# Attention scores in float32r: stacks of two parts on half the TensorE array each, in place of three bf16 parts on the whole array

## The chip, the cores and the metric

The kernel runs on one core of a Trainium2 chip. The metric is the device time of one execution in microseconds (us). Engines are named as in the profile: PE is TensorE's matmul, PEld its weight load, DVE is VectorE, ACT ScalarE, POOL GpSimd, SP SyncE, whose queue issues most DMAs.

## What is computed

The input x holds 64 sequences of 64 channels by 256 positions, in float32. Four residual stages follow each other, each behind a layer norm over the last axis: attention with a band mask (layer 0), a feed-forward with ternary weights and a norm clip (`ff0`), attention with rotary positions on q and k (layer 1), and a feed-forward of width 1024 with 4-bit weights and low-rank terms. The scores of an attention are, shortened:

```python
scores = jnp.einsum('bqhd,bkhd->bhqk', q, k) / jnp.sqrt(jnp.asarray(d, q.dtype))   # 8 heads of d = 8
band = jnp.abs(idx[:, None] - idx[None, :]) <= local_size                          # layer 0: 64
scores = jnp.where(band[None, None], scores, neg)
attn = jax.nn.softmax(scores, axis=-1)
o = jnp.einsum('bhqk,bkhd->bqhd', attn, v).reshape(n, t, e)
```

Layer 1 has the same form over 256 keys without a band, with q and k turned: `t * cos(pos) + rot * sin(pos)`, where `rot` swaps the two halves of each head's 8 channels and negates one.

## The kernel before

Two sequences make a *pair*, laid over the 128 partitions; there are 32 pairs and 16 heads per pair (`HPP`). All of x stays in SBUF (`X`). Each attention layer is one software pipeline over the pairs, written out by hand for each engine: an `iteration(r)` walks the 16 heads of pair r, and beside them works on pairs r+1 (scores and row maxima), r+2 (v, stacks), r+3 (q and k projections) and r-1 (heads turned back, output projection). `Fori` loops run over rounds of `RING` = 3 pairs. Engines are joined by semaphores only, and PE takes its instructions in the order that `tensor_attention.iteration` gives.

Per head the scores are computed twice. `score_head` (L408) computes them with the queries on the partitions, so that DVE takes the row maxima (L1031). `shifted_head` (L425) computes them again with the keys on the partitions and the row maximum subtracted in the same matmul; ACT takes the exponential of that (`exp_head`, L687) into `probs`, and in layer 0 POOL sets the places outside the band to zero (`mask_group`, L1234). `values_group` (L443) multiplies four heads' probabilities with V, in four column strips of the array (L459). In layer 0 a score also starts from a band matmul of 384 columns (L418), which adds a large negative number outside the band. The windows are 192 keys per block of 128 queries in layer 0 (`WIN`), 256 in layer 1.

To keep float32 precision, q and k are split into three bf16 parts (`PARTS` = 3): ACT rounds the first (`high_part`, L699 and L704), DVE takes the rest (L1041) and POOL rounds and subtracts the others (`split`, L1201 to L1208). All nine products of parts are stacked along the contraction: 9 x 8 = 72 rows, and a matmul on `Qs` and `Ks` sums them. The score matmul takes 96 rows (some of them zero), the shifted one 128: rows 96 to 98 hold -1 in `Ks` and the three parts of the row maximum in `Qs`. SP lays the stacks out (`lay_out`, L341 and L344) and replicates them (`replicate`, L355 and L357); `shift_rows` (L366) brings the maxima, which `split_max` (L935 to L941), a transpose on PE (L490) and ACT (L741) have prepared. In layer 1 the rotated rows are taken out of the projection by two ACT instructions of 64 partitions (L716). Four values groups, projections (L470), v (L479), transposes (L501, L512) and the transposes of the maxima (L490) stand between the heads on PE.

At the start of the program the weights of the last feed-forward are prepared on PE by pairs of matmuls that share a bank: 128 rows of dequantised weights, then 16 rows of the low-rank term (L578/L579, L583/L584).

## Time and profile before

| | us |
|---|---|
| median of 3 runs | 1431.23 |
| lowest, highest | 1430.2, 1431.35 |
| profiled execution: span | 1429.4 |
| PE busy | 1315.2 (92%) |
| PEld busy | 910.0 (64%) |
| DVE busy | 955.8 (67%) |
| ACT busy | 874.6 (61%) |
| POOL busy | 716.5 (50%) |

The span runs from the first to the last instruction of the profiled execution, and is the only time shown of that execution. Layer 0 lies between about 45 and 570 us, the first feed-forward up to about 655, layer 1 up to about 1190, the last feed-forward to the end. A busy PE says that matmuls are in flight, not that the array works at its peak; durations of matmuls in the trace include a latency, so the distance from one start to the next tells the cost in a row of them. PEld overlaps PE.

### The profile page before, as it was taken

The page shows a single profiled execution, that of the slowest core. Times are in us where ns is not written, and L with a number is a line of the kernel's source. Part 1 is how long each engine was busy: PE and PEld are TensorE (multiplying, and loading weights), DVE is VectorE, ACT ScalarE, POOL GpSimd, SP SyncE. Part 2 cuts the span into 40 slices and gives each one's busy share as a digit, 9 for nine tenths or more (in the row PEclk, how much of TensorE's full clock was granted, in tenths as well). Part 3 has the DMA queues.
Part 4 walks back from the last instruction along what each step waited for, and adds up shares of the span by engine and source line. Part 5 has one row for each costly group of instructions (what it writes and reads, how often), then busy time and mean ns, then how long its engine had stood idle before and what let it go on. Part 6 is the DMA issues. An engine that isn't in the chain of part 4 may idle for free.

```text
span 1429.4 us, 37785 instructions
## 1 busy us (share of the span) xinstructions
PE 1315.2 (92%) x11332; PEld 910.0 (64%) x11332; DVE 955.8 (67%) x2156; ACT 874.6 (61%) x1909; POOL 716.5 (50%) x1292
## 2 busy tenths in 40 slices
PE   1999999999999998882799999999999989999998
PEld 1666777777777776571466666666666655766675
DVE  6438878787888787468888888888888872111110
ACT  1147676666666667563488888888888875122211
POOL 6336777777777776404555655656656511010000
PEclk9869999999999999995799999999999999999999
DMA  8314444444344443001434444444444410000000
GB/s 243 78 36 95 103 100 90 96 100 100 90 96 100 100 90 87 6 12 37 92 91 104 105 95 103 103 97 104 102 97 107 93 41 1 15 30 15 15 15 29
DMA packets 90797, 111.18 MB, mean 78 GB/s; under 512 B 15056, under 2 KB 82384, under 8 KB 83056
## 3 DMA queue, kind: packets, MB, share of 16 engines
q1 hardware_dynamic: 83184, 103.38, 31.9%
q10 hardware_dynamic: 7552, 7.02, 1.7%
q8 instruction: 34, 0.56, 0.2%
q14 instruction: 27, 0.22, 0.1%
HBM read 16.52 MB, written 4.19 MB: 14 GB/s over the span
## 4 chain that ended last, share of the span: by engine, by line
PE 62%; POOL 11%; issue 11%; DVE 8%; ACT 2%; ACTq 1%; DMA 1%; POOLq 1%; SPq 1%; DVEq 1%
PE bank L459 10%; PE bank L420 8%; PE bank L652 8%; PE bank L643 8%; PE bank L436 7%; PE bank L418 5%; PE bank L470 4%; DVE row_max L1031 3%; PE bank L501 3%; POOL rot L1216 2%; PE bank L614 2%; POOL Qp L1205 2%; PE bank L490 1%; POOL k_rest L1221 1%; POOL q_rest L1201 1%
## 5 line engine op out<-in xcount | busy, mean ns | idle before, releaser
L1031 DVE TENSOR_REDUCE row_max<-bank 128x2 f32<-128x384 f32 (+1 forms) x1024 | 599.6, 617 | 148.5 <-PE bank L420 146.8
L687 ACT ACTIVATE probs<-bank 128x384 f32<-128x384 f32 (+1 forms) x1024 | 534.4, 542 | 161.8 <-PE bank L436 155.0
L420 PE MATMUL bank<-Ks,Qs 96*128 96x192 bf16 (+1 forms) x2048 | 372.1, 264 | 13.5 <-DMA Ks<-Ks 8.4
L436 PE MATMUL bank<-Qs,Ks 128*128 128x192 bf16 (+1 forms) x2048 | 367.1, 261 | 13.6 <-ACT probs L687 12.5
L1234 POOL TENSOR_SCALAR_AFFINE_SELECT probs<-probs 128x256 f32<-128x256 f32 (+1 forms) x512 | 257.2, 526 | 175.1 <-ACT probs L687 156.3
L420 PEld LDWEIGHTS bank<-Ks,Qs 96*128 96x128 bf16 x2048 | 189.3, 99 | 122.8 <-issue 37.8
L459 PE MATMUL bank<-probs,V 128*32 128x192 f32 (+1 forms) x4096 | 249.0, 361 | 3.7 <-POOL probs L1234 2.4
L436 PEld LDWEIGHTS bank<-Qs,Ks 128*128 128x128 bf16 x2048 | 188.9, 98 | 40.1 <-ACT probs L687 23.9
L418 PE MATMUL bank<-band,ident 128*128 128x384 bf16 x512 | 169.2, 331 | 1.0 <-ACT out_bias L840 0.5
L459 PEld LDWEIGHTS bank<-probs,V 128*32 128x32 f32 x4096 | 107.4, 109 | 82.7 <-issue 41.8
L1171 DVE TENSOR_TENSOR X<-bank,X 128x256 f32 (+1 forms) x32 | 13.6, 425 | 184.6 <-PE bank L652 184.6
L1216 POOL TENSOR_TENSOR rot<-rot,rope 128x256 f32<-128x256 f32 x64 | 46.9, 732 | 132.1 <-ACT rot L716 132.1
L643 PE MATMUL bank<-Ks,up_w 128*128 128x512 f32 x256 | 111.8, 592 | 0.0
L1302 POOL TENSOR_TENSOR X<-X,down_b 128x256 f32 x32 | 23.1, 751 | 169.2 <-DVE xn L1006 169.2
L470 PE MATMUL bank<-xn,att_w 128*128 128x256 f32 x192 | 66.2, 431 | 37.7 <-DVE xn L1006 37.7
L733 ACT ACTIVATE heads_sb<-bank 128x512 f32<-128x512 f32 x128 | 75.6, 591 | 27.3 <-PE bank L459 27.3
L643 PEld LDWEIGHTS bank<-Ks,up_w 128*128 128x128 f32 x256 | 48.4, 190 | 56.8 <-issue 56.4
L501 PE MATMUL bank<-ident,heads_sb 128*128 128x128 f32 x512 | 77.9, 275 | 2.0 <-ACT heads_sb L733 2.0
L901 ACT ACTIVATE probs<-bank,up_b 128x512 f32<-128x512 f32 x32 | 22.0, 687 | 85.8 <-PE bank L643 85.8
L716 ACT ACTIVATE rot<-bank,att_b 64x256 f32<-64x256 f32 x128 | 60.0, 469 | 15.2 <-PE bank L470 12.1
L901 ACT ACTIVATE Qs<-bank,up_b 128x512 f32<-128x512 f32 x32 | 22.0, 687 | 76.1 <-PE bank L643 76.1
L501 PEld LDWEIGHTS bank<-ident,heads_sb 128*128 128x128 f32 x512 | 59.2, 142 | 12.3 <-issue 4.4
(128 smaller groups left out, 1776.9 us busy)
## 6 DMA issues: line engine op xcount, KB each, us to landing
Ks<-Ks SPq DMA_DIRECT2D x64, 576.0 KB
Qs<-Qs SPq DMA_DIRECT2D x128, 192.0 KB
Qs<-Qp SPq DMA_DIRECT2D x192, 64.0 KB
Ks<-Kp SPq DMA_DIRECT2D x192, 64.0 KB
side<-in_ctx SPq DMA_DIRECT2D x64, 128.0 KB, 2.0
X<-in_x ACTq DMA_DIRECT2D x4, 1024.0 KB, 10.4
out<-X SPq DMA_DIRECT2D x8, 512.0 KB, 2.9
Qs<-max_rows SPq DMA_DIRECT2D x128, 12.0 KB
```

The source lines that it names most:

```text
L418: nc.tensor.matmul(dst[:, 0:2 * win], ident16[:, :], band16[:, :], start=True, stop=False)
L420: last = nc.tensor.matmul(dst[:, blk * win:(blk + 1) * win], Qs[0:SHIFT_ROW, pair[1], h, blk * P:(blk + 1) * P], Ks[0:SHIFT_ROW, pair[1], ...
L436: last = nc.tensor.matmul(dst[:, blk * win:(blk + 1) * win], Ks[:, pair[1], h, blk * P:(blk + 1) * P], Qs[:, pair[1], h, start(blk):start( ...
L459: last = nc.tensor.matmul(dst[32 * j:32 * j + 32, first:first + win], V[:, pair[1], blk, head, :], probs[:, head % 8, blk * win:(blk + 1) ...
L470: nc.tensor.matmul(job_bank[b][:, 0:T], w[:, weight, :], source, start=True, stop=True).then_inc(s[f"{b}_filled"], 1)
L501: last = nc.tensor.transpose(job_bank["A"][:, (blk * 2 + g) * P:(blk * 2 + g + 1) * P], heads_sb[:, half, g * T + blk * P:g * T + (blk + 1 ...
L643: last = nc.tensor.matmul(bank[2 + hb % 2][:, :], up_w[:, blk, hb * P:(hb + 1) * P], xT[:, cu, blk, :], start=(blk == 0), stop=(blk == 1))
L652: last = nc.tensor.matmul(bank[4 + j % 2][:, 0:T], hidden[cu][:, hb, j * P:(j + 1) * P], down_w[:, hb, :], start=(hb == 0), stop=(hb == HB ...
L687: nc.scalar.activation(probs[:, h % 8, 0:2 * win], exp_bank[h % 2][:, 0:2 * win], ACT.Exp, scale=SCALE).then_inc(s["exped"], 1)
L733: nc.scalar.activation(heads_sb[:, half, :], pv_bank[:, :], ACT.Copy).then_inc(s["heads_out"], 1)
L1031: nc.vector.tensor_reduce(row_max[:, pair[1], h, :], bank_of(pair, h)[:, 0:2 * win].rearrange("p (b k) -> p b k", b=2), AX.X, ALU.max).the ...
L1234: return nc.gpsimd.affine_select(out=part, in_=part, compare_op=ALU.is_ge, fill=0.0, base=base, pattern=[[0, 4], [-sign, width]], channel_ ...
```

## The change

1. `PARTS` is 2: q and k are split into a first part, rounded to float32r on writing (11 mantissa bits are kept), and the rest in float32. The four products of parts take 4 x 8 = 32 rows. An even head and an odd head now share a slot of `Qs` and `Ks` (float32r, eight slots a pair): even heads in partitions 0 to 63, odd heads in 64 to 127. The last two rows of each half (62 and 63) hold -1 in `Ks` and the two parts of the row maximum in `Qs`.
2. A score block takes 62 rows and a shifted block 64 rows of one half. `score_and_shift` issues them block by block in turn, the score of head h of the next pair and the shifted scores of head h^1 of this pair, so that they lie in different halves. Before the first block PE waits for DVE's maxima and for ACT's exponential together. ACT and the values groups follow the swapped order.
3. The stacks are laid out by eight DMAs of 128 KB, spread over the partitions, and `replicate` is gone; `shift_rows` takes two DMAs a half pair. In layer 0 the DMAs wait for the reading of the projection, without POOL's `split`. `Ks` is cleared to -1 by one memset, and POOL's memset of its shift rows is gone.
4. The split of the maxima has two instructions in place of four and moves in layer 0 from DVE to POOL; its transpose is float32 with 32 columns in place of bf16 with 48.
5. In layer 1 a second projection per q and k gives the rotated rows (two more weight blocks), and ACT takes them out with one instruction of 128 partitions in place of two of 64.
6. Buffers of the later stages are other aliases of memory.

On PE in layer 0, two heads in the middle of a pair (L418/L433 the band, L420/L410 the score, L436/L419 the shifted scores, L501/L510 transposes). Before:

```order
L418 MATMUL bank1<-band16,ident16 128x384
L420 MATMUL bank1<-Ks,Qs 128x192 x2
L436 MATMUL bank2<-Qs,Ks 128x192 x2
L501 MATMUL bank6<-ident,heads_sb 128x128 x4
L418 MATMUL bank5<-band16,ident16 128x384
L420 MATMUL bank5<-Ks,Qs 128x192 x2
L436 MATMUL bank3<-Qs,Ks 128x192 x2
```

And in the changed kernel, around a values group (L466) and a transpose of the maxima (L499):

```order
L433 MATMUL bank5<-band16,ident16 128x384
L410 MATMUL bank5<-Ks,Qs 128x192
L419 MATMUL bank3<-Qs,Ks 128x192
L410 MATMUL bank5<-Ks,Qs 128x192
L419 MATMUL bank3<-Qs,Ks 128x192
L466 MATMUL bank4<-probs,V 32x192 x8
L499 MATMUL bank6<-ident,max_parts 32x128
L433 MATMUL bank0<-band16,ident16 128x384
L410 MATMUL bank0<-Ks,Qs 128x192
L419 MATMUL bank2<-Qs,Ks 128x192
```

The number of matmuls per head is the same; the four blocks alternate, and the band matmul stands between the groups of four as before.

On SP, one iteration in the loop of layer 0 (`Qp`, `Kp` are the parts, `max_rows` the turned maxima). Before:

```order
L325 DMA side<-in_ctx 128x256
L341 DMA Qs<-Qp 8x16x256 x3
L344 DMA Ks<-Kp 8x16x256 x3
L366 DMA Qs<-max_rows 3x16x128
L355 DMA Qs<-Qs 24x4096 x2
L357 DMA Ks<-Ks 72x1x4096
L366 DMA Qs<-max_rows 3x16x128
```

And now, with the instructions that take the waits:

```order
L326 DMA side<-in_ctx 128x256
L301 REGISTER_ALU
L301 ISA
L334 DMA Qs<-Qp 16x8x256 x4
L301 REGISTER_ALU
L334 DMA Ks<-Kp 16x8x256 x4
L283 ISA
L364 DMA Qs<-max_rows 2x8x128 x2
L283 REGISTER_ALU
L364 DMA Qs<-max_rows 2x8x128 x2
```

Eight DMAs now stand ahead of the first shift rows in place of six, and none between the two sets of shift rows in place of three.

The core of the diff:

```diff
-PARTS = 3
-SPLIT_ROWS = PARTS * PARTS * HD
-SHIFT_ROW = 96
+PARTS = 2
+SLOTS = HPP // 2
+GROUP = P // 2
+ROWS_D = GROUP // HD
+SHIFT_ROW = GROUP - PARTS
...
-        Qs = sb("Qs", [P, RING, HPP, T], bf16)
-        Ks = sb("Ks", [P, RING, HPP, T], bf16)
+        Qs = sb("Qs", [P, RING, SLOTS, T], fp32r)
+        Ks = sb("Ks", [P, RING, SLOTS, T], fp32r)
...
+            def spread(tensor, u, product, part):
+                dst = bass.AP(tensor, u * SLOTS * T + product * row, [[ROWS_D * row, 2 * HD], [T, SLOTS], [1, T]])
+                return e.dma_start(dst, part)
...
                 for i in range(PARTS):
-                    e.dma_start(Ks[COPY_ROW + i * HD:COPY_ROW + (i + 1) * HD, u, :, :],
-                                Kp[:, u, i, :]).then_inc(s[f"k_in{u}"], 16)
-
-            def replicate(pair):
...
+                    for j in range(PARTS):
+                        spread(q_stack, u, i * PARTS + j, Qp[:, u, i, :]).then_inc(s[f"q_in{u}"], 16)
...
-                e.dma_start(Qs[SHIFT_ROW:SHIFT_ROW + PARTS, pair[1], half * HEADS:(half + 1) * HEADS, :],
-                            max_rows[:, half, :]).then_inc(s[f"max_in{half}"], 16)
+                for odd in range(2):
+                    first = odd * GROUP + SHIFT_ROW
+                    e.dma_start(Qs[first:first + PARTS, pair[1], half * SLOTS // 2:(half + 1) * SLOTS // 2, :]
+                                .bitcast(fp32),
+                                max_rows[odd * PARTS * HEADS:(odd + 1) * PARTS * HEADS, half, :]
+                                ).then_inc(s[f"max_in{half}"], 16)
...
+            def score_block(pair, h, blk):
+
+                rows = slice(h % 2 * GROUP, h % 2 * GROUP + SHIFT_ROW)
+                return nc.tensor.matmul(bank_of(pair, h)[:, blk * win:(blk + 1) * win],
+                                        Qs[rows, pair[1], h // 2, blk * P:(blk + 1) * P],
+                                        Ks[rows, pair[1], h // 2, start(blk):start(blk) + win],
+                                        start=(l == 1), stop=(l == 1 or blk == 1))
+
+            def shifted_block(pair, i, blk):
+
+                h = i ^ 1
+                rows = slice(h % 2 * GROUP, h % 2 * GROUP + GROUP)
+                return nc.tensor.matmul(exp_bank[i % 2][:, blk * win:(blk + 1) * win],
...
+            def score_and_shift(ahead, pair, h):
...
+                    wait_some(e, s["exped"], n - 1)
+                if active(ahead):
+                    score_block(ahead, h, 0)
+                if active(pair):
+                    shifted_block(pair, h, 0)
+                if active(ahead):
+                    score_block(ahead, h, 1).then_inc(s["scored"], 1)
+                if active(pair):
+                    shifted_block(pair, h, 1).then_inc(s["shifted"], 1)
...
+                if turned is not None:
+                    nc.tensor.matmul(job_bank[b][:, T:2 * T], w[:, turned, :], source, start=True, stop=True)
...
-                half = P // 2
-                for here, there in ((slice(0, half), slice(half, P)), (slice(half, P), slice(0, half))):
-                    nc.scalar.activation(rot[here, 2 * n + 1, :], job_bank[bk][there, 0:T], ACT.Identity,
-                                         bias=b[there, column:column + 1]).then_inc(s["turned"], 1)
+                nc.scalar.activation(rot[:, 2 * n + 1, :], job_bank[bk][:, T:2 * T], ACT.Identity,
+                                     bias=b[:, column:column + 1]).then_inc(s["turned"], 1)
...
+            engine.tensor_scalar(parts[:, :, 0, :].bitcast(fp32r), src, 1.0, None, ALU.mult).then_inc(high, 1)
+            wait_apart(e, (high, num(pair) + 1))
+            engine.tensor_tensor(parts[:, :, 1, :], src, parts[:, :, 0, :],
                                  ALU.subtract).then_inc(s[f"max_parts{half}"], 1)
...
-            def split(name, pair, parts, rest, mid, done):
+            def low_part(name, pair, parts, rest):
```

## Rows read from the trace of the kernel before

**Rows 1.** The page, busy time of each engine with its share and instructions.

```profile
span 1429.4 us, 37785 instructions
...
PE 1315.2 (92%) x11332; PEld 910.0 (64%) x11332; DVE 955.8 (67%) x2156; ACT 874.6 (61%) x1909; POOL 716.5 (50%) x1292
```

**Rows 2.** Busy time by stretch: length, engines, granted clock (PEclk), DMA share, GB/s.

```profile
60.00:84.00 24.00, 24.00 (x67) 16.60 (x68) 0.00 (x0) 2.39 (x4) 0.00 (x0) 0.50 0.03 4
202.40:361.40 159.00, 155.02 (x1683) 114.37 (x1682) 127.28 (x332) 109.47 (x250) 117.27 (x211) 1.00 0.43 96
839.40:991.60 152.20, 149.22 (x1502) 99.95 (x1501) 132.14 (x251) 130.11 (x281) 90.59 (x180) 1.00 0.45 101
```

**Rows 3.** The same stretch of layer 0, L436 alone: PE, PEld.

```profile
202.40:361.40 159.00, 52.61 (x322) 28.73 (x320) 1.00 0.43 96
```

**Rows 4.** PE in order of time, layer 0: start, length, line, operands, count.

```profile
303.26 0.32 PE L418 MATMUL bank<-band,ident 128*128 128x384 bf16 x1
303.42 0.33 PE L420 MATMUL bank<-Ks,Qs 96*128 96x192 bf16 x2
303.59 0.33 PE L436 MATMUL bank<-Qs,Ks 128*128 128x192 bf16 x2
303.76 0.32 PE L418 MATMUL bank<-band,ident 128*128 128x384 bf16 x1
...
304.08 0.33 PE L436 MATMUL bank<-Qs,Ks 128*128 128x192 bf16 x2
304.34 0.86 PE L459 MATMUL bank<-probs,V 128*32 128x192 f32 x16
305.13 0.44 PE L512 MATMUL bank<-ident,normed 128*128 128x128 f32 x2
305.41 0.61 PE L479 MATMUL bank<-att_w,xn 128*128 128x128 f32 x4
```

**Rows 5.** PE in order of time, layer 1.

```profile
905.05 0.38 PE L420 MATMUL bank<-Ks,Qs 96*128 96x256 bf16 x2
905.27 0.38 PE L436 MATMUL bank<-Qs,Ks 128*128 128x256 bf16 x2
905.58 1.07 PE L459 MATMUL bank<-probs,V 128*32 128x256 f32 x16
906.58 0.39 PE L420 MATMUL bank<-Ks,Qs 96*128 96x256 bf16 x2
```

**Rows 6.** PE's waits: us in total, times, longest.

```profile
PE bank L420 <- DMA Ks<-Ks: 8.4, 1, 8.4
```

**Rows 7.** PE in order of time, preparation of weights.

```profile
66.32 0.80 PE L583 MATMUL bank<-ident,ff 128*128 128x128 f32 x2
67.04 0.79 PE L584 MATMUL bank<-probs 16*128 16x128 f32 x2
```

**Rows 8.** Groups of weight loads by form: busy us, mean ns of one.

```profile
L420 PEld LDWEIGHTS bank<-Ks,Qs 96*128 96x128 bf16 x2048 | 189.3, 99 | 122.8 <-issue 37.8 <-DVE row_max L1031 11.5 <-DMA Ks<-Ks 8.7
...
L643 PEld LDWEIGHTS bank<-Ks,up_w 128*128 128x128 f32 x256 | 48.4, 190 | 56.8 <-issue 56.4
```

**Rows 9.** SP's queue in order of time, layer 1, one iteration.

```profile
899.96 2.02 SPq L341 DMA_DIRECT2D Qs<-Qp  x3
902.02 1.93 SPq L344 DMA_DIRECT2D Ks<-Kp  x3
904.09 0.77 SPq L366 DMA_DIRECT2D Qs<-max_rows  x1
```

**Rows 10.** PE in the same iteration, the ninth head's shifted scores.

```profile
907.92 0.38 PE L436 MATMUL bank<-Qs,Ks 128*128 128x256 bf16 x2
```

**Rows 11.** The page, DMA issues: count, KB each, median us to landing.

```profile
side<-in_ctx SPq DMA_DIRECT2D x64, 128.0 KB, 2.0
```

**Rows 12.** The chain that ended last, ahead of layer 1's first score.

```profile
664.60 0.91 POOL Qp L1205
...
665.59 0.67 POOL Qp L1208
...
674.43 6.06 DMA Ks<-Ks
```

243 lines of the change are left out of this document (98 added, 145 removed).

## The prediction

> **What bounds the kernel now.** I read the page's busy line first [rows 1]: PE is busy for 92% of the span, no other engine for more than 67%. The table by stretches [rows 2] splits that. Its last two stretches hold ten pairs each (in the first 320 weight loads of L436, 32 a pair [rows 3]), so a pair takes 15.90 us in layer 0 and 15.22 in layer 1. PE is busy for 97% and 98% of them, at full granted clock. Behind it stand DVE with 12.7 us a pair in layer 0 and 13.2 in layer 1, and ACT with 10.9 and 13.0. Then I read PE in order of time. In layer 0 the band matmul comes every 0.50 us: 0.16 for its 384 columns, 0.17 for the two score matmuls, 0.17 for the two shifted ones, nothing between [rows 4]. In layer 1 two matmuls of 256 columns take 0.22, a head 0.44 [rows 5]. That is one column a cycle at 2.4 GHz. The longest wait of a score matmul on anything is a single one of 8.4 us, at a ramp [rows 6]. So what shortens or lengthens PE's row decides, until DVE's 13.2 us or the SP queue takes over.
>
> **The score and shifted matmuls.** Each now uses half the rows, and the order puts a score block on one half beside a shifted block on the other. No row shows a float32r matmul, nor two row halves at once, so I bound them. Plain f32 with 256 columns takes two instructions of 0.216 us (L459's sixteen run in four rounds of four, from 905.58 to 906.46 [rows 5]). If that is four products of operand parts, one product is a quarter, 0.108, as bf16. The same rounds show four matmuls in disjoint column strips running together. If row halves do so too, a head's two block pairs take 0.22 in layer 1 against 0.44, and 0.16 to 0.19 in layer 0 against 0.335. If either fails it is twice that. I take the good case, since L459's rounds are the nearest rows; the bad case is a rival.
>
> **Changing the array's form.** When PE goes from full-array matmuls to L459's 32 columns and back, the next instruction comes late. In layer 0 the last L436 pair starts at 304.08 and lasts 0.17, so L459 was due at 304.25 and starts at 304.34: 0.09 lost. Its rounds of 0.16 end at 304.99 and L512 starts at 305.13 (0.14 lost); its two then take 0.28 where two of L479 take 0.22 (0.06, a weight load that nothing hides) [rows 4]. In layer 1 it is 0.09 in and 0.12 out [rows 5]. The preparation shows it for rows: f32 matmuls alternate between 128 and 16 rows at a granted clock of 0.50, 1.2 GHz [rows 2], and come every 0.72 us [rows 7], where two of L479's 0.11 at half speed are 0.44; the other 0.28 is one change of form. The bf16 stacks of 96 and 128 rows alternate without loss [rows 4]; a half of 62 or 64 rows I count as a form of its own.
>
> So in layer 0 each head now leaves and enters that form, because its band matmul is full-array. Out: 0.09, and 0.01 for a bf16 load. In: 0.09, and an exposed float32r load. A bf16 load lasts 99 ns, an f32 one 190 [rows 8]. I bound the exposed part by 0.05 (L512's) and 0.11 (the excess of 0.09 on top of a bf16 load's 0.01 to 0.02), and take 0.08. The four blocks go from 0.335 to between 0.40 and 0.49 us, middle 0.445: +0.11 a head, +1.8 us a pair, **+55 us** over 31 pairs; the ends are +32 and +77.
>
> The Trainium skill, page "TensorE: Matmul & The Clock Gate", section "Weight-path perf modes", says that weights load fast when there are 128 of them and the input is not FP32; the 99 against 190 ns agrees. An estimate by it: if float32r counts as FP32 this term takes its upper end, +77; if it loads as bf16 does, exposed 0.01, it is +12.
>
> In layer 1 there is no band, but projections, transposes and values groups stand between the heads. Along the loop's order I count 20 changes of form a pair against 11 before (the transpose of the maxima now has the values group's 32 columns). That is 9 x 0.09 = +0.8, and ten entries with a load of 0.08, less the bf16 loads, +0.7. Blocks: 16 x 0.22 = -3.5. The rotated projections are two more f32 matmuls, four instructions of 0.216: +0.9. Sum -1.1 us, a pair of 14.1, still above DVE's 13.2. ACT's four half-height L716 become two full ones, off the path.
>
> **What moves on SP.** The stacks now take eight DMAs and no replication. Three L341 took 2.02 us to issue and three L344 1.93 [rows 9], so about 0.65 each. Behind them queues the shift row of the second half, now two DMAs. Before, it was issued 4.13 us after the iteration began (899.96 to 904.09 [rows 9]) and used at 907.92, the ninth head [rows 10]. Now its second DMA is issued after 8 x 0.65 + 0.77 = 6.0 us, and with the 2.0 us that the side load takes to land [rows 11] it is there at 8.0, when layer 1's ninth head is due at 7.96 - 0.55 = 7.4. PE waits 0.5 or so. The landing takes 3.8 us at most (904.09 to 907.92, with no wait), the wait then 2.4. In layer 0, with 17.7 us a pair, the head is due near 8.8: no wait. Layer 1: -1.1 + 0.5 = -0.6 a pair, **-18 us** over 30, ends -33 and +39.
>
> **The ramps.** In the chain before layer 1's first score [rows 12], POOL's L1205 and L1208 go, for q and for k (2 x 1.58 = 3.2 us), and the replication's 6.06; the larger layout DMAs give back some 2. With 3 at the program's start: **-10 us**, ends -15 and -5. Costed at nothing: DVE's split of the maxima in layer 0 moves to POOL, which loses 1.6 us of work each for q and k and gains four small operations. It stands there behind a mask group with about one head to spare before PE asks; without that, PE would wait for it once a pair. The changed aliases of the later stages move no work.
>
> **Sum.** The profiled execution's span is 1429.4 us [rows 1], the runs' median 1431.2, so 1.8 lies around the span. 1429.4 + 55 - 18 - 10 = 1456.4, and 1.8 more: **1458 us**. Its own range, by the ends and +12 as the lowest first term, is 1395 to 1540.
>
> **Rivals.**
> - *Changing form costs little here*, for instance since one half works while the other drains. Layer 0's blocks fall to 0.175: -0.16 x 16 x 31 = -79. Layer 1 loses the added 1.5 too, but its first half cannot go below SP's 8.0 us, so I give it -1.0 x 30 = -30. With the ramps **1312**. The balance point: my gains elsewhere are 28 us, 0.056 a head of layer 0, so the kernel is faster if a way out and in costs under 0.22 us, where I take 0.27. For it: L459 in layer 1 shows 0.21. Against it: the preparation pays in full, by rows.
> - *A four-byte moving operand streams at half speed.* Every f32 instruction in the rows takes two cycles a column, transposes too (L512, 0.28 less 0.06 for two of 128). Blocks then double: +0.17 x 16 x 31 = +84 and +3.5 x 30 = +105, less the SP wait's 15, on the forecast: **1632**. The skill's page "SBUF — State Buffer", section "A bandwidth-pool intuition that's wrong (but worth ruling out)", gives the moving operand's port as two bytes a lane and cycle, which is this rule.
> - *The change doesn't do what it says*: the halves run one after the other, each block 0.08 or 0.11. Same doubled price, **1632**. L459's overlap is in columns; no row shows one in rows.
> - *A lower clock.* In the preparation the clock stayed at 0.50 while forms alternated [rows 2]. If it did so in layer 0, a head's 0.33 us of columns would double and its two changes cost 0.28 each: +0.6 us, some +300 over 31 pairs. PE streams a larger share there, so I give it little.
>
> **Chances.** Forecast 0.55, of which 0.14 end faster (cheap end of the form change) and 0.04 the same; cheap changes 0.15; half speed 0.13; no overlap 0.12; lower clock 0.05. Faster 0.29, same 0.04 (within 0.2%, what a measurement of this kernel can tell from no change), slower 0.67. The range runs from 1380 to 1640: the forecast's own and both doubled prices. Outside lie most of the cheap case and the lower clock, 0.19.
>
> **What would show it.** In layer 0: band matmuls 0.6 us apart instead of 0.50, with 0.09 lost before and after the blocks; the two blocks of a pair starting a few ns apart, the next two 0.08 to 0.11 later. A spacing of 0.16 there is half speed; four evenly spaced starts are no overlap. Pairs of 17.7 us in layer 0 and 14.6 in layer 1, and there a wait of the ninth shifted head for the max_rows DMA. I am wrong if the band's spacing stays at 0.50 or below, or if a pair of layer 1 takes over 15.2.

## The result and the profile after

The changed kernel takes **1536.11 us** (median of four runs, 1535.57 to 1537.6) against 1430.72 us for the kernel before on the same chip. The ratio is 1.074, with a 95% interval of 1.0724 to 1.0755: slower by 105 us, where I had forecast 27. The profiled execution's span goes from 1429.4 to 1535.7 us. The page of the changed kernel, against [rows 1]:

```profile
span 1535.7 us, 37561 instructions
...
PE 1433.7 (93%) x11460; PEld 903.6 (59%) x11460; DVE 901.9 (59%) x1900; ACT 849.6 (55%) x1845; POOL 524.1 (34%) x1035
```

PE took the whole loss: it is busy 118 us longer, and every other engine is busy for less than before, POOL by 192 us. The busy time by stretch, against [rows 2] (length, PE, PEld, DVE, ACT, POOL, granted clock, DMA share, GB/s):

```profile
200.00:380.00 180.00, 178.40 (x1688) 106.91 (x1690) 113.10 (x252) 111.43 (x251) 96.23 (x210) 1.00 0.25 67
640.00:700.00 60.00, 53.55 (x383) 31.10 (x382) 20.98 (x53) 29.18 (x62) 25.52 (x54) 0.67 0.02 7
900.00:1100.00 200.00, 196.40 (x2000) 125.50 (x1998) 169.71 (x325) 156.67 (x338) 69.75 (x130) 1.00 0.29 79
```

PE is as full as before in both layers (99% and 98%), at full clock. New is the middle row, the end of layer 0: a granted clock of 0.67. PE in order of time in layer 0 of the changed kernel, against [rows 4] (start, length, line, operands, count):

```profile
305.05 0.34 PE L433 MATMUL bank<-band,ident 128*128 128x384 bf16 x1
305.32 0.35 PE L410 MATMUL bank<-Ks,Qs 62*128 62x192 f32 x1
305.32 0.35 PE L419 MATMUL bank<-Qs,Ks 64*128 64x192 f32 x1
305.51 0.27 PE L410 MATMUL bank<-Ks,Qs 62*128 62x192 f32 x1
305.52 0.27 PE L419 MATMUL bank<-Qs,Ks 64*128 64x192 f32 x1
305.72 0.48 PE L479 MATMUL bank<-rot,att_w 128*128 128x256 f32 x1
```

The two halves do overlap: score and shifted block start together, and the second pair of blocks is done 0.20 us after its start. What is paid lies between the instructions. The band matmul streams for 0.16 us and the blocks begin 0.27 after it (0.11 lost). A block pair is 192 columns, 0.08 at one column a cycle of 2.4 GHz, and the next follows after 0.19 (0.11 lost). After the second, the next full-array matmul starts 0.20 later (0.12 lost). So a head takes 0.16 + 0.11 + 0.08 + 0.11 + 0.08 + 0.12 = 0.66 us where it took 0.50. The weight loads of that head show the middle loss:

```profile
305.32 0.18 PEld L410 LDWEIGHTS bank<-Ks,Qs 62*128 62x128 f32 x1 [0.17 <-issue]
305.32 0.18 PEld L419 LDWEIGHTS bank<-Qs,Ks 64*128 64x128 f32 x1
305.43 0.19 PEld L410 LDWEIGHTS bank<-Ks,Qs 62*128 62x128 f32 x1
```

A float32r load lasts 0.18 to 0.19 us, as the f32 load of [rows 8], and the second load on the same half comes 0.11 after the first.

To place the rest I took from both traces the start of the first shifted matmul of some pairs, which cuts the span into stretches:

| stretch | before, us | after, us | difference |
|---|---|---|---|
| start to pair 0 of layer 0 | 90.2 | 108.0 | +17.8 |
| pair 0 to 4 | 64.4 | 75.3 | +10.9 |
| pair 4 to 31 | 431.1 | 492.1 | +61.0 |
| pair 31 to first transpose of `ff0` | 15.2 | 21.5 | +6.3 |
| to pair 0 of layer 1 | 92.8 | 92.2 | -0.6 |
| pair 0 to 4 | 69.3 | 71.6 | +2.3 |
| pair 4 to 31 | 415.1 | 420.8 | +5.7 |
| rest | 251.3 | 254.3 | +3.0 |

Between pairs 4 and 30 a pair takes 17.91 us in layer 0 (before 15.87) and 15.48 in layer 1 (before 15.21). The steady price is 31 x 2.04 = 63 us in layer 0 and 30 x 0.27 = 8 in layer 1. The other 35 us lie at the ramps: 17.8 before the first pair, 2.7 in the next four beyond their steady price, 12.2 at the end of layer 0 (5.9 of it in the row of pairs 4 to 31), and 2.4 elsewhere. (The 570 us given above for the end of layer 0 is too early. In the kernel before, its last scores stand at 584.5 us and its last shifted matmul starts at 596.7.)

The ramps show two things, a lower clock and changes of form that cost more at it. PE in order of time while layer 0's first pair is scored, first the changed kernel:

```profile
53.55 0.50 PE L433 MATMUL bank<-band,ident 128*128 128x384 bf16 x1
53.98 0.74 PE L410 MATMUL bank<-Ks,Qs 62*128 62x192 f32 x2
54.65 0.50 PE L433 MATMUL bank<-band,ident 128*128 128x384 bf16 x1
```

and the kernel before in the same phase:

```profile
52.65 0.34 PE L418 MATMUL bank<-band,ident 128*128 128x384 bf16 x1
52.83 0.33 PE L420 MATMUL bank<-Ks,Qs 96*128 96x192 bf16 x2
53.12 0.34 PE L418 MATMUL bank<-band,ident 128*128 128x384 bf16 x1
```

A head is 1.10 us there instead of 0.47. The blocks begin 0.43 us after the band matmul, whose 384 columns are 0.32 us at the 1.2 GHz level and 0.16 at 2.4. The clock is the smaller part of the 0.63 us, because a little earlier the kernel before scores at that level too:

```profile
47.96 0.53 PE L418 MATMUL bank<-band,ident 128*128 128x384 bf16 x1
48.28 0.53 PE L420 MATMUL bank<-Ks,Qs 96*128 96x192 bf16 x2
48.60 0.97 PE L470 MATMUL bank<-xn,att_w 128*128 128x256 f32 x2
```

Its head takes 0.64 us (47.96 to 48.60). The other 0.46 of the 1.10 come with the change's blocks: the changes of form and the exposed load at half clock. In the trace of before the clock is granted at 1.00 from 49.3 to 59.5 us and again from 93.7; in the changed kernel first from 121.2. At the end of layer 0 it falls to 0.50 from 653.7 to 674.2 and twice more up to 701.5, where before it was lost for 3.4 us only.

### The profile page after: what moved, and what is told of

Read it like the earlier page. It is cut to its first block, busy times and chain, and to the rows that moved or that the text cites. A ratio compares the mean times of both kernels' runs of the same rounds, so it can differ in the third digit from the quotient of the medians.

```text
span 1535.7 us, 37561 instructions
## 1 busy us (share of the span) xinstructions
PE 1433.7 (93%) x11460; PEld 903.6 (59%) x11460; DVE 901.9 (59%) x1900; ACT 849.6 (55%) x1845; POOL 524.1 (34%) x1035
## 4 chain that ended last, share of the span: by engine, by line
PE 82%; DVE 6%; POOL 4%; issue 3%; ACT 3%; ACTq 1%; SPq 0%; POOLq 0%; DVEq 0%; DMA 0%
PE bank L410 20%; PE bank L466 14%; PE bank L661 7%; PE bank L479 7%; PE bank L652 7%; PE bank L433 6%; PE bank L510 4%; POOL probs L1221 3%; PE bank L419 3%; PE bank L478 2%; DVE row_max L1035 2%; PE bank L488 2%; PE bank L623 2%; PE bank L521 2%; ACT probs L697 1%
## 5 line engine op out<-in xcount | busy, mean ns | idle before, releaser
L410 PE MATMUL bank<-Ks,Qs 62*128 62x192 f32 (+1 forms) x2048 | 467.9, 322 | 28.4 <-ACT probs L697 14.2
L419 PE MATMUL bank<-Qs,Ks 64*128 64x192 f32 (+1 forms) x2048 | 461.1, 320 | 2.4 <-ACT probs L697 2.4
L410 PEld LDWEIGHTS bank<-Ks,Qs 62*128 62x128 f32 x2048 | 305.8, 192 | 249.2 <-issue 134.5
L419 PEld LDWEIGHTS bank<-Qs,Ks 64*128 64x128 f32 x2048 | 299.2, 190 | 8.8 <-ACT probs L697 6.4
L466 PE MATMUL bank<-probs,V 128*32 128x192 f32 (+1 forms) x4096 | 253.9, 367 | 7.8 <-POOL probs L1221 4.4
L433 PE MATMUL bank<-band,ident 128*128 128x384 bf16 x512 | 176.2, 344 | 0.5 <-ACT out_bias L848 0.5
L466 PEld LDWEIGHTS bank<-probs,V 128*32 128x32 f32 x4096 | 108.7, 111 | 72.4 <-POOL probs L1221 8.2
L943 POOL TENSOR_SCALAR max_parts<-row_max 128x16 fp32r<-128x16 f32 x128 | 32.5, 254 | 345.0 <-DVE row_max L1035 339.7
L909 ACT ACTIVATE ff<-bank,up_b 128x512 f32<-128x512 f32 x64 | 44.0, 687 | 163.5 <-PE bank L652 163.5
L661 PE MATMUL bank<-down_w,ff 128*128 128x256 f32 x512 | 112.6, 381 | 0.8 <-ACT ff L909 0.8
L652 PE MATMUL bank<-probs,up_w 128*128 128x512 f32 x256 | 112.7, 597 | 0.0
L661 PEld LDWEIGHTS bank<-down_w,ff 128*128 128x128 f32 x512 | 96.6, 190 | 15.8 <-ACT ff L909 1.6
L510 PE MATMUL bank<-ident,heads_sb 128*128 128x128 f32 x512 | 82.8, 285 | 1.6 <-ACT heads_sb L741 1.4
L652 PEld LDWEIGHTS bank<-probs,up_w 128*128 128x128 f32 x256 | 48.8, 192 | 57.7 <-issue 57.3
## 6 DMA issues: line engine op xcount, KB each, us to landing
ff<-in_down_q ACTq DMA_DIRECT2D x1, 1024.0 KB, 10.8
```

The lines of the kernel that those rows point to most:

```text
L410: return nc.tensor.matmul(bank_of(pair, h)[:, blk * win:(blk + 1) * win], Qs[rows, pair[1], h // 2, blk * P:(blk + 1) * P], Ks[rows, pair[ ...
L419: return nc.tensor.matmul(exp_bank[i % 2][:, blk * win:(blk + 1) * win], Ks[rows, pair[1], h // 2, blk * P:(blk + 1) * P], Qs[rows, pair[1 ...
L433: nc.tensor.matmul(bank_of(ahead, h)[:, 0:2 * win], ident16[:, :], band16[:, :], start=True, stop=False)
L466: last = nc.tensor.matmul(dst[32 * j:32 * j + 32, first:first + win], V[:, pair[1], blk, head, :], probs[:, head % 8, blk * win:(blk + 1) ...
L510: last = nc.tensor.transpose(job_bank["A"][:, (blk * 2 + g) * P:(blk * 2 + g + 1) * P], heads_sb[:, half, g * T + blk * P:g * T + (blk + 1 ...
L652: last = nc.tensor.matmul(bank[2 + hb % 2][:, :], up_w[:, blk, hb * P:(hb + 1) * P], xT[:, cu, blk, :], start=(blk == 0), stop=(blk == 1))
```

## The experiments

My theory was that the loss is made of changes of form (the array emptied before and after the blocks, and a four-byte load that nothing hides) and of lost clock at the ramps. The rivals: the half-array float32r blocks are slow by themselves; the load has no part in it; the ramps are long for another reason. "Pair" below is the time between pairs 4 and 30 in the profiled run, divided by 26, as above.

### 1. Without the band matmul

```diff
-                    if l == 0:
-                        nc.tensor.matmul(bank_of(ahead, h)[:, 0:2 * win], ident16[:, :], band16[:, :],
-                                         start=True, stop=False)
...
-                                        start=(l == 1), stop=(l == 1 or blk == 1))
+                                        start=True, stop=True)
```

> The changed kernel without the layer 0 band matmul (left out: the mask in the scores of layer 0, so that its row maximum is taken over the whole window). Theory, form changes: each change of form costs a drain of about 0.11 us and an exposed load of about 0.1 us; without the band the half-array pairs follow each other as in layer 1 (spacing 0.12 us) and a head falls from 0.66 to 0.24-0.30 us, a layer 0 pair from 17.97 to 12-13.5 us, where VectorE (11.3 us a pair) is near; time about 1536 - 31 x 5 = 1380 us (1360 to 1410). Rival, the float32r blocks themselves are slow (0.19 us for two halves whatever stands before them): a head stays at 0.38 us or more, a pair at 13.5-15 us, time 1430 to 1470 us.

Measured: 1542.95 us, ratio 1.0781 (1.0739 to 1.0822). Less work, and no gain. The table by stretches of this kernel says why; the first row is layer 0's steady part, the others two pieces of it:

```profile
200.00:380.00 180.00, 163.01 (x1459) 106.15 (x1458) 105.50 (x240) 100.58 (x241) 90.72 (x201) 0.79 0.23 63
330.70:340.90 10.20, 8.51 (x104) 5.63 (x102) 7.64 (x17) 6.75 (x17) 5.77 (x13) 1.00 0.33 84
341.00:368.00 27.00, 26.72 (x170) 16.78 (x162) 12.00 (x27) 12.38 (x28) 10.91 (x24) 0.50 0.21 57
```

The clock alternates between its two levels all through layer 0. DVE has 11.1 us of work a pair here (105.50 us in 180, a pair being 19.02). At full clock it does 7.64 us in 10.20, so a pair takes 15; at half clock 12.00 in 27, so 25. Where the clock is full, the blocks behave as the theory says:

```profile
371.41 0.35 PE L410 MATMUL bank<-Ks,Qs 62*128 62x192 f32 x1
...
371.60 0.27 PE L410 MATMUL bank<-Ks,Qs 62*128 62x192 f32 x1
371.60 0.38 PE L419 MATMUL bank<-Qs,Ks 64*128 64x192 f32 x2
371.72 0.27 PE L410 MATMUL bank<-Ks,Qs 62*128 62x192 f32 x1
...
371.83 0.27 PE L410 MATMUL bank<-Ks,Qs 62*128 62x192 f32 x1
```

After the change of form the second block pair comes 0.19 later, the third and fourth 0.11 to 0.12: the load is exposed once per entry and hidden from then on. The theory holds for the blocks, and my forecast of the time missed by 160 us. Most of that is the clock, which it left out, but not all: even at full clock a pair took 15 us, with PE busy for 8.51 of 10.20 us, where my 1380 us needs 12.9. By an estimate from these rows that is 31 x 2.1 = 65 of the 160.

### 2. The same in the kernel before

> The kernel before without the layer 0 band matmul (left out: the mask in the scores of layer 0). Here every matmul of a head has the full form, so only the band's own 0.16 us can go: a pair falls by 16 x 0.16 = 2.6 us from 15.89 to 13.3 us, the time by 31 x 2.6 = 80 us to 1350 us (1340 to 1365). If a band matmul cost more than its stream in this kernel too, the fall is over 100 us and the comparison with the changed kernel does not show form changes.

The edit is the same, on L418 and L420. Measured: 1392.22 us, ratio 0.9734 (0.9716 to 0.9752), **faster than both kernels**, and 42 us above my forecast. A pair falls by 1.26 us and not by 2.56, since PE now waits (146.41 us busy of 160, against 155.02 of 159 [rows 2]). The clock is at 1.00 from 116.7 to 540.0 us. So the band can go without losing the clock where the other matmuls fill the whole array.

### 3. The halves with bf16 loads

```diff
+            def rows_of(h):
+                return slice(h % 2 * 64, h % 2 * 64 + 64)
...
-                                            Qs[0:SHIFT_ROW, pair[1], h, blk * P:(blk + 1) * P],
-                                            Ks[0:SHIFT_ROW, pair[1], h, start(blk):start(blk) + win],
+                                        Qs[rows_of(h), pair[1], h, blk * P:(blk + 1) * P],
+                                        Ks[rows_of(h), pair[1], h, start(blk):start(blk) + win],
```

(the shifted blocks take `rows_of(h + 1)`; order and waits are those of the change)

> The kernel before with its blocks cut to 64 rows of the array and issued block by block between the halves as in the change (left out: the products in the other half of the stacks). Theory, form change = drain + four-byte load: the drain of 0.11 us stays twice a head, the exposed load (bf16 loads take 99 ns instead of 190) goes down to 0.05 us or less: a layer 0 head of 0.50-0.58 us, a pair of 15.5-16.7 us. Rival, the exposed load does not depend on the type: a head of 0.65 us and a pair of 17.9 us as in the changed kernel. Rival, only the load costs: a head below 0.40 us and a pair under 14.5 us.

Measured, in one execution: 1435.75 us, a pair of 16.21 us in layer 0 and 14.62 in layer 1. PE in order of time, layer 0 of this kernel:

```profile
303.93 0.33 PE L433 MATMUL bank<-band,ident 128*128 128x384 bf16 x1
304.19 0.25 PE L413 MATMUL bank<-Ks,Qs 64*128 64x192 bf16 x1
304.19 0.25 PE L420 MATMUL bank<-Qs,Ks 64*128 64x192 bf16 x1
304.28 0.24 PE L413 MATMUL bank<-Ks,Qs 64*128 64x192 bf16 x1
...
304.46 0.34 PE L433 MATMUL bank<-band,ident 128*128 128x384 bf16 x1
```

and its weight loads of the next head:

```profile
304.72 0.09 PEld L413 LDWEIGHTS bank<-Ks,Qs 64*128 64x128 bf16 x1 [0.17 <-issue]
304.73 0.09 PEld L420 LDWEIGHTS bank<-Qs,Ks 64*128 64x128 bf16 x1
304.74 0.10 PEld L413 LDWEIGHTS bank<-Ks,Qs 64*128 64x128 bf16 x1
```

The 0.10 before and the 0.10 after the blocks are there, but the second block pair follows after 0.09 instead of 0.19, and the second load on a half comes 0.02 after the first instead of 0.11. A head takes 0.53 us. So changes of form alone cost layer 0 0.34 us a pair over the kernel before, because the overlapped blocks pay for them; the other 1.70 us of the change's 2.04 come with the float32r stacks, and the exposed load is most of it (16 x 0.11 = 1.8, where every head has one). A small part of that difference may be the rest of the change, since this kernel keeps the three-part splits on the other engines.

Its start is long as well. Pair 0's first shifted matmul stands at 100.0 us (90.2 before, 108.0 with the change), the clock is first granted at 104.2, and the scores of the first pair take 16.5 us (10.5 before, 20.2 with the change). So more than half of what the start loses comes without float32r.

### 4. More full-array work at the ramps

```diff
+                        times = 3 if not active(pair) else 2 if isinstance(pair[0], int) and num(pair) == 0 else 1
+                        for t in range(times):
                             nc.tensor.matmul(bank_of(ahead, h)[:, 0:2 * win], ident16[:, :], band16[:, :],
-                                             start=True, stop=False)
+                                             start=True, stop=t < times - 1)
...
+                elif l == 0 and h > 3 and active(pair):
+                    e.wait_ge(s["maxed"], PAIRS * HPP)
+                    for _ in range(2):
+                        nc.tensor.matmul(score_bank[h % 2][:, 0:2 * win], ident16[:, :], band16[:, :],
+                                         start=True, stop=True)
```

> The changed kernel with its band matmul issued three times a head in layer 0's score-only iterations, twice in the first iteration that also shifts, and two extra band matmuls a head into idle score banks in layer 0's last iteration: full-array work in the stretches where the granted clock was low. Nothing is left out. Theory, the ramps are lost by the clock: the clock is granted at 1.00 by the first pair's scores or soon after 105 us instead of at 121, and does not fall at 653 us; 20 to 40 us come back, time 1496 to 1520 us. Rival, the ramps are long because half-array heads are longer there at either clock: no gain, 1536 to 1545 us, since the extra matmuls only add work.

Measured: 1541.4 us, the median of four executions of which one took 4035.23 us (why isn't known) and the others 1535.96 to 1543.42; the span of the profiled one is 1534.1. The clock moved but the time did not. It was granted from 62.6 us to 76.2, in the weight preparation, again from 124.0 to 137.7, and came to stay at 141.1 instead of 121.2; from pair 0 to 4 took 80.3 us. At the end of layer 0 it stayed at 1.00 until 694.0, and pairs 4 to 31 took 483.5 us instead of 492.1. Those 8.6 us come with the clock, but it isn't shown that the extra matmuls kept it: the profiled executions of experiments 9 and 11, whose layer 0 is that of the change word for word, kept it to 680.3 and 671.0 us and took 483.7 both. As a test of the ramps the experiment is inconclusive.

### 5. Score, score, shifted, shifted

```diff
                 if active(ahead):
                     score_block(ahead, h, 0)
-                if active(pair):
-                    shifted_block(pair, h, 0)
-                if active(ahead):
                     score_block(ahead, h, 1).then_inc(s["scored"], 1)
                 if active(pair):
+                    shifted_block(pair, h, 0)
                     shifted_block(pair, h, 1).then_inc(s["shifted"], 1)
```

> The changed kernel with a head's four blocks in the order score, score, shifted, shifted instead of alternating. Theory, two halves overlap only where consecutive matmuls stand in different halves, and a load on one half hides behind a stream on the other: a layer 0 head grows by 0.05 to 0.15 us (pair 18.8-20.4 us), a layer 1 head by 0.1-0.2 us (pair 17-18.5 us), time 1610 to 1690 us. Rival, the array takes the next half's load early whatever the order: same time within 10 us.

Measured, in one execution: 1536.03 us, a pair of 17.94 and 15.53 us. The rival was right. PE in order of time in this kernel:

```profile
304.40 0.33 PE L433 MATMUL bank<-band,ident 128*128 128x384 bf16 x1
304.65 0.35 PE L410 MATMUL bank<-Ks,Qs 62*128 62x192 f32 x1
304.66 0.35 PE L419 MATMUL bank<-Qs,Ks 64*128 64x192 f32 x1
304.85 0.27 PE L410 MATMUL bank<-Ks,Qs 62*128 62x192 f32 x1
```

The first shifted block starts beside the first score block although two score blocks stand before it in the program. It starts 7 ns after it and not 3 (medians from 200 to 380 us), the only mark that the new order left. Alternating block by block, which the change wrote out with care, does nothing for the time; that the blocks lie in different halves does all.

This run also gives a price for the clock by chance: here it was granted at 143.6 us instead of 121.2, and pairs 0 to 4 took 83.9 us instead of 75.3; it was kept until 662.4, and pairs 4 to 31 took 485.7 instead of 492.1, the way to `ff0` 16.9 instead of 21.5. The edit changes no steady pair, so 22 us at half clock at the start cost 8.6, and the fall at the end of layer 0 cost 11. The moment of the grant needn't be the edit's doing. With layer 0 as in the change, it came at 121.4 us in experiment 11 (pairs 0 to 4 in 75.8 us) and at 144.5 in experiment 9 (84.0 us). So how the 35 us are spread over the ramps belongs in part to the one execution that was profiled; the four executions of the change lie within 2.1 us of each other.

### 6. Half-array work twice

```diff
+                for blk in range(2):
+                    for rep in range(2 if l == 0 and active(ahead) and active(pair) else 1):
+                        if active(ahead):
+                            scored = score_block(ahead, h, blk)
+                        if active(pair):
+                            shifted = shifted_block(pair, h, blk)
```

> The kernel without bands (left out: the mask in the scores of layer 0), with every half-array block of layer 0 issued twice in place: more work, the same form. Without bands the granted clock alternated between 0.50 and 1.00 all through layer 0 and a pair took 19.1 us (about 15 at 1.00, 25 at 0.50). Theory, the clock is granted for how much the array does: with the doubled blocks it stays at 1.00, a head costs 4 x 0.12 = 0.48 us and a pair 15.5-17 us, time 1543 - 31 x 2.5 = 1465 us (1440 to 1500), faster with more work. Rival, the clock answers to full-array forms alone or the pair is bound elsewhere: the clock goes on alternating and the time rises to 1600-1680 us.

Measured: 1513.74 us, ratio 1.057 (1.0485 to 1.0656). Against experiment 1 it does twice the block work and is 29 us **faster**. The table by stretches of this kernel:

```profile
200.00:380.00 180.00, 173.83 (x2202) 128.21 (x2194) 110.85 (x255) 109.46 (x254) 98.25 (x214) 1.00 0.26 70
```

The clock is held. A pair takes 17.59 us, over the 17 I had allowed, so the time lies above my range. Half-array work keeps the clock too, if there is enough of it.

### 7. A band matmul only where the form is full anyway

```diff
-                    if l == 0:
+                    if l == 0 and h in (0, 1, 4, 5, 8, 10, 12, 14):
                         nc.tensor.matmul(bank_of(ahead, h)[:, 0:2 * win], ident16[:, :], band16[:, :],
-                                         start=True, stop=False)
+                                         start=True, stop=True)
```

> The kernel without bands (left out: the mask in the scores of layer 0), with one band matmul, whose result is overwritten, at 8 of the 16 heads of layer 0: only where a full-array job or the values matmuls stand before it, so that no change of form is added. It is 8 x 0.16 = 1.3 us a pair more work than without bands (19.1 us a pair, clock 0.50 half of the time). Theory, full-array work holds the granted clock: clock 1.00 through layer 0, a pair of 15-16.5 us, time 1543 - 31 x 3.4 = 1438 us (1420 to 1470). Rival, half the bands are too few: the clock falls again and again and the time stays over 1500 us.

Measured: 1486.26 us, ratio 1.0375 (1.0341 to 1.0409): 57 us less than experiment 1, with eight useless matmuls a pair added. Layer 0's steady part in this kernel:

```profile
200.00:380.00 180.00, 162.52 (x1728) 104.28 (x1728) 117.95 (x273) 111.97 (x271) 103.71 (x227) 0.99 0.28 74
```

PE is busy for as long as in experiment 1 (163.01), but at 0.99 instead of 0.79, and does 10.8 pairs in it instead of 9.5. A pair takes 16.62 us. The rest to my 1438 us is waiting: PE idles for 10% of the stretch, behind POOL's mask (10.0 us, 11 times) and ACT. With experiment 6 this shows the clock as the main cause of experiment 1's result, and PE's slack does not mean that a pair could be shorter.

### 8. Bands for two heads at once

```diff
-                    wait_some(e, s["maxed"], n - SCORE_BANKS + 1)
-                    if l == 0:
-                        nc.tensor.matmul(bank_of(ahead, h)[:, 0:2 * win], ident16[:, :], band16[:, :],
-                                         start=True, stop=False)
+                    if l == 1 or h % 2 == 1:
+                        wait_some(e, s["maxed"], n - SCORE_BANKS + 1)
+                    if l == 0 and h % 2 == 0:
+                        for k in range(2):
+                            wait_some(e, s["maxed"], n + k - SCORE_BANKS + 1)
+                            nc.tensor.matmul(bank_of(ahead, h + k)[:, 0:2 * win], ident16[:, :], band16[:, :],
+                                             start=True, stop=False)
...
-                    if h == 3:
+                    if h == (3 if l else 2):
                         turn_max("B", r, 1)
```

(the query projection moves from head 1 to 2 and `turn_heads(m1, 1)` from 5 to 6 in the same way)

> The changed kernel with layer 0's band matmuls issued for two heads at once and three jobs (row-maximum transpose, query projection, a heads transpose) moved by one head beside them, so that a pair has 8 excursions out of the half-array form fewer; nothing is left out and no matmul is added. Theory: an excursion costs two drains of 0.10 us and one exposed four-byte load of 0.10-0.12 us, so 8 x 0.3 = 2.4 us a pair come back, layer 0 pair 15.6 us, time 1536 - 31 x 2.4 = 1462 us (1450 to 1480). Rival, the granted clock answers to full-array work and bands placed two and two are not enough: it falls in layer 0 as it did without bands, and the time stays above 1520 us.

Measured: 1474.32 us, ratio 1.0303 (1.0218 to 1.0388): 62 us of the 105 are back, with the same matmuls. PE in order of time, two heads of this kernel:

```profile
303.33 0.49 PE L436 MATMUL bank<-band,ident 128*128 128x384 bf16 x2
303.75 0.35 PE L410 MATMUL bank<-Ks,Qs 62*128 62x192 f32 x1
...
303.95 0.27 PE L410 MATMUL bank<-Ks,Qs 62*128 62x192 f32 x1
...
304.06 0.27 PE L410 MATMUL bank<-Ks,Qs 62*128 62x192 f32 x1
...
304.17 0.27 PE L410 MATMUL bank<-Ks,Qs 62*128 62x192 f32 x1
304.37 0.66 PE L513 MATMUL bank<-ident,heads_sb 128*128 128x128 f32 x4
```

Two heads take 1.04 us (303.33 to 304.37) instead of 1.32: 0.28 for one excursion out of the half-array form and back, as said. Eight of them are 2.2 us of PE's work; a pair became 1.43 us shorter (16.48), the rest turned into waits (PE 95% busy instead of 99%). The start shared in it: pair 0 to 4 and the way there took 166.1 us instead of 183.3, with the clock granted from 55.1 to 65.3 and again from 109.7; and at the end of layer 0 it was lost for 3.4 us only.

### 9 and 10. More excursions in layer 1, and their control

```diff
+                    if l == 1 and h in (7, 9, 11, 13):
+                        nc.tensor.matmul(bank_of(ahead, h)[:, 0:16], ident16[:, :], band16[:, 0:16],
+                                         start=True, stop=True)
```

> The changed kernel with one tiny full-array matmul (16 columns, bf16, into a score bank that is then overwritten) before the score blocks of heads 7, 9, 11 and 13 of layer 1: four more excursions out of the half-array form a pair and almost no streaming; nothing is left out. Theory: 0.3 us each on a TensorE that is 98% busy, 4 x 0.3 x 31 = 37 us, time 1573 us (1560 to 1580), layer 1 pair 16.8 us. Rival, layer 1's end is set by the chain through VectorE and ScalarE and the form is cheap there: under 10 us.

> The control: the same four tiny matmuls a pair in layer 1 of the kernel before, whose blocks all have the full form, so that no form changes with them. Theory: only an extra weight load and 16 columns each, 0.02 to 0.1 us, 2 to 12 us in all (1431 to 1441 us). If this costs as much as in the changed kernel, an excursion's price is that of a matmul and not of the form.

Measured: 1550.96 us in the changed kernel (1537.84 to 1555.87, ratio 1.0837, 1.0771 to 1.0904; in the profiled executions the two rows of layer 1's pairs are 10.9 us longer than in the change, a pair 15.81 against 15.48), and 1432.55 us in the kernel before, ratio 1.0016 (1.0006 to 1.0026), a pair 15.22 against 15.21. The control is clear: where no form changes, four tiny matmuls cost nothing that a pair shows. The price in the changed kernel is 0.33 us a pair, far under the 1.2 I expected, and the placement was part of my error: the values matmuls stand before heads 7 and 11, so those two were no new excursions. A new one, ahead of head 9 or 13:

```profile
1000.39 0.28 PE L419 MATMUL bank<-Qs,Ks 64*128 64x256 f32 x1
1000.60 0.18 PE L433 MATMUL bank<-band,ident 128*128 128x16 bf16 x1
1000.75 0.38 PE L410 MATMUL bank<-Ks,Qs 62*128 62x256 f32 x1
```

The next blocks start 0.36 after the last ones instead of 0.12: 0.24. Two of them a pair are 0.5; PE went from 98% to 100% busy (200.00 of 200 us), which absorbs 0.3.

### 11. The rotated projections twice

```diff
                 if turned is not None:
-                    nc.tensor.matmul(job_bank[b][:, T:2 * T], w[:, turned, :], source, start=True, stop=True)
+                    for _ in range(2):
+                        nc.tensor.matmul(job_bank[b][:, T:2 * T], w[:, turned, :], source, start=True, stop=True)
```

> The changed kernel with the two rotated projections of layer 1 issued twice each (same result). The prediction put their cost at 0.9 us a pair, all on TensorE's path. Theory: layer 1 is bound by TensorE, so another 0.9 to 1.1 us a pair, 28 to 34 us, time 1564 to 1570 us. Rival, part of it lies in waits: 5 to 15 us.

Measured: 1558.8 us (1548.39 to 1564.34), ratio 1.0914 (1.0885 to 1.0943), a pair of layer 1 16.25 us: +0.77 us, a little under what I expected. The profiled execution is the shortest of the four: its two rows of layer 1's pairs are 22.1 us longer than in the change, but pairs 4 to 31 of layer 0 took 483.7 us instead of 492.1. On PE, q's projections with the turned one take 1.06 us from the first start to the next group where experiment 3 has 0.65 for one, and k's 0.97 where it has 0.54: 0.85 a pair. So the term was rightly sized at 0.9, with a little of it absorbed.

### 12. Jobs of layer 1 moved together

```diff
-                    if h == 1:
+                    if h == (3 if l else 1):
                         project("A", "q", p3, WQ, xn[:, p3[1], :],
...
-                    if h == 4 + l:
+                    if h == (7 if l else 4):
                         project("B", "k", p3, WK,
```

(and `turn_heads(m1, 1)` from 5 to 7, the output projection from 10 to 11, `turn_heads(r, 0)` from 14 to 15, in layer 1)

> The changed kernel with four jobs of layer 1 (query and key projection, a heads transpose, output projection, the other heads transpose) moved one or two heads later so that they stand beside the values matmuls: 6 excursions out of the half-array form a pair instead of 10, nothing left out. Theory, layer 1 is bound by TensorE and an excursion costs 0.3 us: 4 x 0.3 = 1.2 us a pair, 30 pairs, 1536 - 36 = 1500 us (1490 to 1515). Rival, layer 1 is bound by the chain through VectorE (13 us busy a pair): under 8 us of gain, or a loss where a job comes later than its reader wants it.

Measured: 1730.69 us, ratio 1.2083 (1.1987 to 1.2179): 195 us worse than the change. It says nothing of the forms, since PE was busy for only 78% of layer 1. The waits of layer 1 in this kernel, 950 to 1150 us (total, times, longest):

```profile
DVE rcp L1064 <- PE bank L510: 49.3, 19, 5.0
ACT rot L724 <- PE bank L479: 48.8, 18, 4.4
```

DVE, ACT and POOL execute their instructions in a written order that has these results in it at fixed places. A job that PE delivers two heads late holds DVE for 2.6 us on average, with PE's next score behind it. Which of the moves does it wasn't tried apart.

### 13. GpSimd's dequantising held back

```diff
+            e.wait_ge(L[0]["xn_ready"], 3)
             dequantise(e, nc.gpsimd, up_f, up_raw, up_scale, HB * T // QBLOCK, dequant_up)
```

> The changed kernel with GpSimd's dequantising (which the change let start at 21.2 us, where GpSimd split parts before) held back until three pairs are normalised; nothing is left out. Theory: VectorE's first normalise takes 0.4 us instead of 4.0 because GpSimd's 5.4 us pass over 2048 columns no longer runs beside it, and the program's start comes forward by 3 to 5 us; time 1531 to 1533 us, unless the granted clock rises at another moment. Rival, VectorE's 4 us come from something else: no change in that row.

Measured: 1529.48 us, ratio 1.0705 (1.0682 to 1.0728), 6.6 us less than the change. The first normalise in the changed kernel, with the POOL pass beside it:

```profile
22.70 4.01 DVE L1010 TENSOR_SCALAR xn<-X,mean,rstd 128x256 f32<-128x256 f32 x1
```

```profile
21.20 5.37 POOL L927 TENSOR_SCALAR ff<-ff 128x2048 f32<-128x2048 int32 x1 [12.26 <-DMA probs<-in_lora_out]
```

and in this kernel, where the pass runs from 34.38 on:

```profile
23.16 0.41 DVE L1010 TENSOR_SCALAR xn<-X,mean,rstd 128x256 f32<-128x256 f32 x1
```

The normalise in the changed kernel ends 0.14 us after the pass (26.71 against 26.57). The kernel before has the same collision, but with its third normalise, while POOL's pass runs from 31.21:

```profile
32.99 3.73 DVE L1006 TENSOR_SCALAR xn<-X,mean,rstd 128x256 f32<-128x256 f32 x1
```

Taking the splits away from POOL let it start the pass 10 us earlier, and so moved the collision to the first normalise, for which PE waits. Layer 0's pair 0 comes 4.3 us sooner without that. The rest of the gain in the profiled execution lies at the end of layer 0, where the clock was lost for 3.4 us at 652.5, instead of for 20.5 us at 653.7.

### 14. Experiments 8 and 13 together

> The best forms of the change together, nothing left out: bands for two heads at once with the three moved jobs (1474 us) and GpSimd's dequantising held back (-7 us). If the two are independent: 1467 us (1462 to 1472), with the first normalise at 0.4 us. If the ramp is set by the moment at which the clock is granted and not by the late start, nothing is added to the 1474 us.

Measured: 1467.28 us, ratio 1.0255 (1.0235 to 1.0274). By the medians they add up, as expected. The two profiled executions don't show it (spans of 1469.9 and 1468.7 us): the scores begin 4.4 us sooner here, but the clock was first granted at 106.4 us and not at 55.1. It is the best form of the change that I found, still 2.5% slower than the kernel before; experiment 2 is 2.7% faster than it.

## Why the prediction was wrong

The direction and the range held, the size did not. That 1536 lies even in the forecast's own range, 1395 to 1540, is luck: the ramps came out 40 us beyond the worse end that I gave them, and the other two terms left the room by staying under theirs. One of my signs of being wrong came true, a pair of layer 1 over 15.2. By its steps:

- **Score and shifted blocks**: right. Halves overlap, a block pair of 256 columns comes every 0.12 us in a run, and no float32r block runs at half speed. A pair of 192 columns comes every 0.11 too, so the 0.08 that I took for it in layer 0 is never reached in a row. The rivals "half speed" and "the halves run one after the other" fall. The rule of the Trainium skill, page "SBUF — State Buffer", section "A bandwidth-pool intuition that's wrong (but worth ruling out)", that the moving port gives two bytes a lane and cycle (its figure is for bf16), is not what float32r shows here: 256 columns of four bytes in 0.12 us, over both halves.
- **Changing the array's form in layer 0**: the mechanism was right and its parts were small by a little. Out 0.12 instead of 0.10, in 0.11 instead of 0.09, exposed load 0.11 instead of 0.08: 0.34 a head instead of 0.27. A pair cost +2.04 us instead of +1.8 (less than 16 times the excess of 0.16, since beside the values matmuls and jobs the form changed before too): +63 us where I had +55. The Trainium skill, page "TensorE: Matmul & The Clock Gate", section "Weight-path perf modes", gives fast loads only to inputs other than FP32. By the 0.18 to 0.19 us of its loads float32r behaves as FP32 does, and of the two ends that I worked out from that rule (+12 and +77) the upper one is the near one.
- **Layer 1**: wrong in sign, +8 us where I had -18. The failed step is "blocks: 16 x 0.22 = -3.5" with "9 x 0.09 = +0.8" for the changes. In experiment 3, which has the halves and the changes but neither float32r nor the second projections, PE's own work is 136.25 us in 150, 13.3 a pair; before it was 14.9 (149.22 of 152.20 [rows 2]). That is -1.6 where I had -2.7. A block pair in a run takes 0.12 and not 0.107 (16 x 2 x 0.012 = 0.4). Another 0.4 the traces place where I had nothing: a full-array f32 job behind half-array blocks has its own load exposed. The second matmul of a projection starts 0.32 us after the first (0.22 to 0.24 before; three a pair), that of a transpose 0.165 (0.108 before; two a pair). I had read this 0.06 off L512 [rows 4] and counted it for the blocks alone. The last 0.3 is open. The exposed loads were +1.1 instead of +0.7 (ten at 0.11), the rotated projections right at 0.9. Together 13.3 + 1.1 + 0.9 = 15.3, and PE's work in the changed kernel is 98% of 15.48 = 15.2. DVE's 13.2 was no floor to reckon with either: experiment 3's pair stood at 14.62 with PE 91% and DVE 88% busy.
- **SP's queue**: the expected wait did not come. In layer 1's steady part PE idles for 3.6 us in 200, and the one wait that its table shows is on ACT's exponential (3.3 us). That was 0.5 us a pair too much, on the other side.
- **Ramps**: this is the step that failed most, +35 us where I had -10. I reckoned there with POOL's splits and the replication, and put at nothing what the changes of form cost while the first pair is scored, and the clock. The lower clock stood as a rival in the wrong place: at 0.05, and in layer 0's steady part. There it held. It was low while only scores are computed, in the first iterations after the preparation, and in the last ones, where only shifted blocks are left. Of the 35, 5 are that the first scores begin later (50.3 instead of 45.2 us; POOL's pass is 4.3 of them, experiment 13). Some 10 are the first pair's scores, 20.2 us from the first to the last instead of 10.5. Over half of that is changes of form at half clock: by the rows above 0.46 us a head, 16 x 0.46 = 7, and experiment 14, with the same matmuls, the clock not yet granted and eight bands fewer between the blocks, takes 15.0. Some 11 are the fall of the clock at the end of layer 0 (experiment 5, by comparison), in the execution that was profiled. The remaining 9 I put down to the clock's return at 121.2 us instead of 93.7; experiment 5's price, 8.6 us for 22, fits that, but the one run that tried to give the clock back (experiment 4) could not show it.
- **Sum**: 63 + 8 + 35 = 106, against 55 - 18 - 10 = 27.

## What to carry to other kernels

Splitting the array in halves saves streaming time and costs an emptying and a refilling each time a full-array instruction stands between: 0.24 to 0.28 us an excursion with four-byte weights here, 0.2 with bf16. Before halving, count the excursions, put the full-array jobs together, and leave everything else in the order in which its readers want it. Count the clock with the work: an edit that makes TensorE do less for the same result can lose the full clock, and then an added, useless matmul pays; so read the granted clock of every stretch, the ramps too. And ask first whether the small matmul that forces the change is needed: the band mask in the scores only shapes the row maximum here, because POOL clears the exponentials outside the band anyway and a shift cancels in the softmax. Dropping it from the kernel before is the best version found (1392 us), with one condition: no score outside the band may exceed the row's largest one inside by so much that the exponentials vanish. That condition is argued; no run tried other data.
